# Third norm of a macaron block: two of four tiles scaled by ScalarE, and the next group's additions to x placed ahead of the reciprocals on VectorE

## The chip, the cores and the metric

The kernel runs on one core of one Trainium2 chip. Time is device microseconds of one execution, and the figure of a kernel is the median of its runs. The engines are named as the profile names them: PE is TensorE's matmul stream and PEld its weight loads, DVE is VectorE, ACT is ScalarE, POOL is GpSimd, SP is SyncE. Each engine takes its own instructions strictly in the order in which they were written and waits on semaphores of the others.

## The reference

The input x has 4096 tokens of 256 numbers. Three residual stages follow each other:

```
x = x + 0.5 * moe_ffn(layernorm(x))      # gate, top 2 of 8 experts
x = x + attention(layernorm(x))          # 16 heads, causal
x = x + 0.5 * moe_ffn(layernorm(x))      # the same weights again

layernorm(x) = (x - mean(x)) / sqrt(var(x) + 1e-5)
```

The change is in the third layernorm, the one between the attention and the second pass through the experts. What it computes stays as it is.

## The kernel before

The tokens stand in 32 tiles of 128 (one token per partition), and x stays in SBUF as `x_res`. A norm goes through the tiles in 8 groups of four. In the third norm each group g goes through these steps:

- TensorE projects the heads' output, `attended(g)` on TensorE (line 1484): 16 matmuls of a group, 8 for each of its two pairs of tiles, into banks 4 and 5.
- VectorE adds each pair to x (`attended(g)` on VectorE, which calls `add_pair`, line 1846): two instructions of 128x512. A pair's addition waits for that pair's last matmul.
- VectorE's `statistics` (lines 1514, 1517, 1519): bn_stats and bn_aggr for each of four tiles, then variance plus epsilon for the group.
- ScalarE takes the square root (`sqrt_of`, line 879).
- VectorE's `normalise` takes the reciprocal (line 1524) and scales the four tiles into `rows_of(1)` (line 1536).
- TensorE transposes the four tiles (`transpose_rows`, line 1144): eight transposes, the first feature half of the four tiles and then the second half. ScalarE copies both halves to `feat` (`copy_feat`, line 896).
- TensorE computes the gate logits from `feat` (`gate`, line 1157, 16 matmuls), ScalarE adds the bias (`copy_gate`, line 904), and TensorE turns the logits back (`gate_rows`, line 1166).

The order on TensorE is written out in its `layer_norm`: attended(0), and then for each g attended(g + 1), gate(g - 1), the transposes of g, gate_rows(g - 1). At the end gate(7) and gate_rows(7). On VectorE it is, for each group in turn, additions, statistics, normalise, so that normalise(g) stands ahead of the additions of g + 1. Inside VectorE's `attended` two instructions of the last head's division are written as well: a reciprocal (line 1865) behind the additions of group 1 and a multiplication (line 1869) behind those of group 3. On ScalarE, for each g: copy_gate(g - 1), copy_feat(g), sqrt_of(g + 1).

The first norm has the form that the change brings to the third. There VectorE computes -mean * rstd (line 1527, semaphore `shift`), scales the first two tiles of a group itself, and ScalarE scales the last two (line 922, semaphore `normed_s`) with that value as bias. Behind the third norm `route(1)` chooses the experts, and it needs the gate logits of all groups. SP meanwhile loads the experts' weights, which waits for the last division.

Of the kernel before, what the change touches and what calls it, by code (L numbers as in the profile page):

```python
# [10 lines left out]
ACT = mybir.ActivationFunctionType  # L11
# [5 lines left out]
D = 256  # L17
# [34 lines left out]
LN_GRP = (4, 4, 4)  # L52

BY_SCALAR = 2
# [8 lines left out]
GATES = NT // GATE_TILES  # L63
# [295 lines left out]
def macaron_block(nc, x_in, w_qkv_t, w_out_t, gate_w, gate_b, w1, w2, w3, bias_cols, out):  # L359
    with ExitStack() as ctx:  # L360
        sig = Signals(nc, ctx)

        def sb(name, shape, dt=F32):
            return ctx.enter_context(nc.sbuf_tensor(name, shape, dt))


        x_res = sb("x_res", [P, NT, D])
        rows = sb("rows", [P, NT, ROW])
# [7 lines left out]
        rstd = sb("rstd", [P, 3, NT])  # L376
# [129 lines left out]
        def rows_of(f):  # L506
            return late_rows if f else rows
# [21 lines left out]
        def bc(ap, axis, shape):  # L529
            return ap.unsqueeze(axis).to_broadcast(shape)  # L530
# [4 lines left out]
        s_places, s_steps, S_ALL = bank_places()  # L535
# [326 lines left out]
        def _(eng):  # L862
            need = Waits(eng)
# [12 lines left out]
            def sqrt_of(n, g):  # L876
                a, b = g * LN_GRP[n], (g + 1) * LN_GRP[n]
                need.wait_ge(sig.eps[n], g + 1)
                eng.activation(rstd[:, 1, a:b], rstd[:, 0, a:b], ACT.Sqrt).then_inc(sig.sqrt[n], 1)

            def copy_feat(n, g):

                a, b = g * LN_GRP[n], (g + 1) * LN_GRP[n]
                if n == 1:
                    need.wait_ge(sig.combined[0], 2 * b - NT)
                if n == 2:
                    need.wait_ge(sig.out_mm, b * KD)
                for i0 in range(a, b, 4):
                    for k in range(KD):
                        m = i0 // 4 * KD + k  # L890
                        need.wait_ge(sig.tr[n], 4 * (m + 1))
                        to, of = feat[:, k, i0 * P:(i0 + 4) * P], bank[k][:, :]
                        if n == 1:
                            to = to.rearrange("p (i g b) -> p g i b", i=TPJ, g=TPJ)
                            of = of.rearrange("p (g i b) -> p g i b", i=TPJ, g=TPJ)
                        eng.activation(to, of, ACT.Copy).then_inc(sig.feat[n], 1)
# [10 lines left out]
            def widen_ids(f):  # L907
# [4 lines left out]
                eng.activation(lo_wide[f], bc(lo_ids[:, :], 2, [P, P, HOTS]), ACT.Copy).then_inc(sig.widened[f], 1)  # L912
                eng.activation(hi_wide[f], bc(hi_ids[:, :], 2, [P, N_SUB, HOTS]), ACT.Copy).then_inc(sig.widened[f], 1)

            def first_norm():
                sqrt_of(0, 0)
                for m in range(GATES):
                    if m + 1 < GATES:
                        sqrt_of(0, m + 1)
                    need.wait_ge(sig.shift, m + 1)  # L920
                    for i in range((m + 1) * LN_GRP[0] - BY_SCALAR, (m + 1) * LN_GRP[0]):
                        eng.activation(rows[:, i, 0:D], x_res[:, i, :], ACT.Identity, scale=rstd[:, 0, i:i + 1],
                                       bias=rstd[:, 2, i:i + 1]).then_inc(sig.normed_s, 1)
                    if m:
                        copy_feat(0, m - 1)
                    if m > 1:
                        copy_gate(0, m - 2)
                copy_feat(0, GATES - 1)
                copy_gate(0, GATES - 2)
                copy_gate(0, GATES - 1)  # L930

            def layer_norm(n, add, consume):
                add(0)
                sqrt_of(n, 0)
                groups = NT // LN_GRP[n]
                for g in range(groups):
                    if g + 1 < groups:
                        add(g + 1)
                    if n == 2 and g:
                        copy_gate(1, g - 1)  # L940
                    copy_feat(n, g)
                    if g + 1 < groups:
                        sqrt_of(n, g + 1)
                    consume(g)
                if n == 2:
                    copy_gate(1, GATES - 1)
# [175 lines left out]
        def _(eng):  # L1122
            need = Waits(eng)

            def transpose_rows(n, g):
                need.wait_ge(sig.const, ident_at[0])
                for i0 in range(g * LN_GRP[n], (g + 1) * LN_GRP[n], 4):
                    for k in range(KD):
                        m = i0 // 4 * KD + k
                        need.wait_ge(sig.feat[n], m - 1)  # L1130
                        if n == 1:
                            need.wait_ge(sig.xt_copy[0], DIRECT)
                            need.wait_ge(sig.w_copy, PAIRS)
                        if n == 2:
                            need.wait_ge(sig.s_done, S_ALL)
                        for i in range(i0, i0 + 4):
                            by_vector = LN_GRP[0] - BY_SCALAR
                            if n:
                                need.wait_ge(sig.normed[n], i + 1)
                            elif i - i0 < by_vector:  # L1140
                                need.wait_ge(sig.normed[0], g * by_vector + i - i0 + 1)
                            else:
                                need.wait_ge(sig.normed_s, g * BY_SCALAR + i - i0 - by_vector + 1)
                            eng.transpose(bank[k][:, (i - i0) * P:(i - i0 + 1) * P], rows_of(n // 2)[:, i, k * P:(k + 1) * P],
                                          ident[:, :]).then_inc(sig.tr[n], 1)

# [354 lines left out]
        def _(eng):  # L1501
            need = Waits(eng)

            def statistics(n, g):
                a, b = g * LN_GRP[n], (g + 1) * LN_GRP[n]
                tiles = range(a, b)
                for i in tiles:
                    if n == 0:
                        need.wait_ge(sig.block_loaded[g], 16)
                    elif n == 1:  # L1510
                        need.wait_ge(sig.x_added[0], i // 2 + 1)
                    else:
                        need.wait_ge(sig.attended, i // 2 + 1)
                    eng.bn_stats(stats[:, i, :], x_res[:, i, :]).then_inc(sig.stat[n], 1)  # L1514
                need.wait_ge(sig.stat[n], b)
                for i in tiles:
                    eng.bn_aggr(mean_var[:, i, :], stats[:, i, :]).then_inc(sig.mv[n], 1)
                need.wait_ge(sig.mv[n], b)
                eng.tensor_scalar(rstd[:, 0, a:b], mean_var[:, a:b, 1], EPS, None, ALU.add).then_inc(sig.eps[n], 1)

            def normalise(n, g):
                a, b = g * LN_GRP[n], (g + 1) * LN_GRP[n]
                need.wait_ge(sig.sqrt[n], g + 1)
                eng.reciprocal(rstd[:, 0, a:b], rstd[:, 1, a:b]).then_inc(sig.rstd[n], 1)
                need.wait_ge(sig.rstd[n], g + 1)
                if n == 0:
                    eng.scalar_tensor_tensor(rstd[:, 2, a:b], mean_var[:, a:b, 0], -1.0, rstd[:, 0, a:b], ALU.mult,
                                             ALU.mult).then_inc(sig.shift, 1)
                    b -= BY_SCALAR

                if n == 1:
                    need.wait_ge(sig.table[0], 16 * GROUPS)
                if n == 2:
                    need.wait_ge(sig.s_full, S_ALL)
                for i in range(a, b):
                    eng.tensor_scalar(rows_of(n // 2)[:, i, 0:D], x_res[:, i, :], mean_var[:, i, 0:1], rstd[:, 0, i:i + 1],  # L1536
                                      ALU.subtract, ALU.mult).then_inc(sig.normed[n], 1)
# [8 lines left out]
            def layer_norm(n, add, consume):  # L1546
                add(0)
                statistics(n, 0)
                normalise(n, 0)
                groups = NT // LN_GRP[n]  # L1550
                for g in range(groups):
                    if g + 1 < groups:
                        add(g + 1)
                        statistics(n, g + 1)
                        normalise(n, g + 1)
                    consume(g)

# [379 lines left out]
def bank_places():  # L1937


    places, value, by_place = {}, 0, []  # L1940
    for what, n in attention_steps():
        if what in ("begin_chunk", "probs"):
            value += what != "begin_chunk"
            places[what, n] = len(by_place), value
            by_place.append((what, n))
    return places, by_place, value
# [52 lines left out]
```

## Time and profile before

| | us |
|---|---|
| median of 3 runs | 2087.17 (2084.46 to 2088.4) |
| profiled execution, device time | 2089.44 |
| its span | 2087.7 |
| third norm and its gate, in the span | from 1786 to 1834 |

In the span PE was busy 96% of the time, DVE 88% and ACT 74%. The clock granted to TensorE was 0.975 of full speed in the mean. Instructions are placed in time from the start of the span. A PE instruction's end is modelled and its start is recorded, so the distances between starts are the surer reading. Where a row merges several instructions of one line ("x4"), its duration goes from the first start to the last end, and consecutive instructions overlap slightly.

### The profile page before, as it was taken

Reading aid. Unit: us, or ns where it says so; the run is one execution under the profiler, and the core shown is the slowest. Engines: PE = TensorE matmul, PEld = TensorE weight load, DVE = VectorE, ACT = ScalarE, POOL = GpSimd, SP = SyncE. Lnnn points to the kernel's source line nnn. Section 1 sums busy time; section 2 is a strip of 40 time slices with the busy share of each in tenths; the row PEclk is TensorE's granted clock in tenths of the full one; section 3 lists DMA queues with packets and bytes.
Section 4 is the critical chain, followed back from the end, with each engine's and each line's share of the span. In section 5 each row is a group of like instructions: output and inputs, shape, how many; then the busy total and the mean of one; then the engine's idle time right before and its main releaser. Section 6 shows DMA issues by size and latency. Waiting matters only on the chain.

```text
span 2087.7 us, 99148 instructions
## 1 busy us (share of the span) xinstructions
PE 2005.4 (96%) x43237; PEld 1552.1 (74%) x43237; DVE 1836.2 (88%) x3799; ACT 1545.8 (74%) x3191; POOL 394.2 (19%) x990
## 2 busy tenths in 40 slices
PE   5899989999999999999999999999999999969998
PEld 3788865477777777777777777777877886748885
DVE  6677766899999999999999999999999997667776
ACT  6233346699999999999999999999999998433332
POOL 1343213311111111111111111111111111024330
PEclk8799989999999999999999999999999999969998
DMA  8577603401010010100122001010010102437774
GB/s 273 137 171 172 151 32 122 135 30 37 13 43 21 30 36 12 43 22 29 38 67 72 21 29 37 12 43 22 28 37 12 43 17 67 145 112 176 170 175 131
DMA packets 272403, 154.57 MB, mean 74 GB/s; under 512 B 160142, under 2 KB 253984, under 8 KB 271968
## 3 DMA queue, kind: packets, MB, share of 16 engines
q1 hardware_dynamic: 258764, 119.63, 21.1%
q0 software_dynamic: 6816, 19.20, 3.5%
q10 hardware_dynamic: 6388, 9.39, 1.7%
q8 instruction: 339, 5.55, 1.1%
q14 instruction: 96, 0.79, 0.1%
HBM read 96.98 MB, written 50.93 MB: 71 GB/s over the span
## 4 chain that ended last, share of the span: by engine, by line
PE 82%; DVE 9%; issue 3%; DMA 2%; ACT 1%; POOL 1%; SPq 1%; another core or an unknown queue 0%; DVEq 0%; ACTq 0%; POOLq 0%
PE bank L1387 38%; PE bank L1380 21%; PE bank L1259 16%; PE bank L1469 3%; DVE work L1905 2%; DVE stats L1514 1%; PE bank L1430 1%; DVE x_res L1846 1%; DMA phase<-head_reciprocals 1%; DVE work L1536 0%; POOL phase L660 0%; DVE work L1806 0%; PE bank L1340 0%; POOL work L660 0%
## 5 line engine op out<-in xcount | busy, mean ns | idle before, releaser
L1102 ACT ACTIVATE feat<-bank 128x512 f32<-128x512 f32 (+3 forms) x2304 | 1263.8, 565 | 117.5 <-PE bank L1387 18.1
L1387 PE MATMUL bank<-work 96*32 96x512 bf16 (+2 forms) x15872 | 1211.5, 370 | 7.1 <-DVE work L1905 6.0
L1905 DVE TENSOR_REDUCE work<-bank 128x1 f32<-128x512 f32 (+1 forms) x1920 | 1185.7, 664 | 33.1 <-PE bank L1387 29.4
L1380 PE MATMUL bank<-feat,phase 128*17 128x128 f32 (+3 forms) x18432 | 888.1, 263 | 1.4 <-issue 1.2
L1380 PEld LDWEIGHTS bank<-feat,phase 128*17 128x17 f32 x18432 | 603.0, 98 | 258.8 <-ACT feat L1108 15.7
L1387 PEld LDWEIGHTS bank<-work 96*32 96x32 bf16 (+1 forms) x15872 | 482.3, 96 | 60.0 <-DVE work L1905 26.4
L1259 PE MATMUL bank<-work 128*128 128x256 f32 (+1 forms) x1872 | 384.1, 364 | 11.2 <-ACT work L1008 6.1
L1259 PEld LDWEIGHTS bank<-work 128*128 128x128 f32 x1872 | 329.8, 191 | 60.4 <-issue 15.3
L694 POOL TENSOR_SCALAR_AFFINE_SELECT feat<-feat 128x128 f32<-128x128 f32 x512 | 147.3, 296 | 660.0 <-ACT feat L1102 640.8
L647 POOL DMA_INDIRECT work<-token_table,row_no x142 | 149.9, 1056 | 258.2 <-DVE work L1783 163.1
L1767 DVE COPY work<-phase 128x514 f32 x234 | 101.1, 434 | 82.0 <-ACT work L1008 41.7
L1469 PE MATMUL bank<-work 98*32 98x256 bf16 (+11 forms) x2560 | 171.3, 258 | 0.2 <-ACT feat L1102 0.2
L1008 ACT ACTIVATE work<-bank,work 128x256 f32<-128x256 f32 (+1 forms) x156 | 62.5, 451 | 137.3 <-PE bank L1259 116.9
L685 POOL CAST work<-work 128x4 bf16<-128x4 f32 x128 | 24.0, 188 | 524.5 <-DVE work L1911 522.4
L975 ACT ACTIVATE work<-work 128x256 f32<-128x256 f32 (+1 forms) x156 | 60.6, 389 | 82.3 <-DVE work L1797 70.7
L1469 PEld LDWEIGHTS bank<-work 98*32 98x32 bf16 x2560 | 88.8, 95 | 4.8 <-ACT feat L1102 2.1
L1896 DVE TENSOR_REDUCE work<-bank 128x4 f32<-128x512 f32 x128 | 88.1, 688 | 0.0
L1901 DVE TENSOR_REDUCE work<-bank 128x4 f32<-128x512 f32 x128 | 87.5, 684 | 0.0
L1806 DVE TENSOR_SCALAR work<-bank,work 128x256 f32<-128x256 f32 (+1 forms) x156 | 64.5, 454 | 22.1 <-PE bank L1259 12.6
L1797 DVE SCALAR_TENSOR_TENSOR work<-bank,work 128x256 f32<-128x256 f32 (+1 forms) x156 | 64.3, 453 | 13.3 <-PE bank L1259 10.5
L1430 PEld LDWEIGHTS bank<-work 96*32 96x32 bf16 x2048 | 43.3, 96 | 12.3 <-issue 2.6
L1788 DVE STREAM_TRANSPOSE work<-rows 128x512 f32<-128x512 f32 (+1 forms) x70 | 46.1, 659 | 0.4 <-DMA rows<-tile_rows 0.4
(210 smaller groups left out, 1119.1 us busy)
## 6 DMA issues: line engine op xcount, KB each, us to landing
tile_rows<-work SPq DMA_DIRECT2D x128, 128.0 KB
rows<-tile_rows SPq DMA_DIRECT2D x232, 64.0 KB
phase<-in_w SPq DMA_DIRECT2D x12, 1024.0 KB, 11.9
work<-qk_parts SPq DMA_DIRECT2D x60, 192.0 KB
work<-work SPq DMA_DIRECT2D x512, 0.5 KB
head_sums<-feat SPq DMA_DIRECT2D x128, 64.0 KB
qk_parts<-phase SPq DMA_DIRECT2D x20, 384.0 KB, 2.7
work<-qk_parts SPq DMA_DIRECT2D x60, 128.0 KB
```

The source lines that it names most:

```text
L647: eng.indirect_dma_start(out=x_slot[:, j % NXG, u, :], out_offset=None, in_=table[f], in_offset=bass.IndirectOffsetOnAxis(ap=row_no[:, n:n ...
L694: eng.affine_select(out=tile, in_=tile, compare_op=ALU.is_ge, fill=0.0, base=0, pattern=[[way, P]], channel_multiplier=-way).then_inc(sig. ...
L1102: eng.activation(p_ring[:, n % P_RING, lo:QB], s_bank("probs", n)[:, lo:QB], ACT.Exp, scale=HD ** -0.5).then_inc(sig.s_done, 1)
L1259: mm = eng.matmul(bank[bk][:, m * TILE:m * TILE + WIDTH[j]], staged[:, b, l, k * D + m * P:k * D + (m + 1) * P], act, start=(k == 0), stop ...
L1380: mm = eng.matmul(bank[ACC_BANK][GRID * g:GRID * g + VW, GRID * i0:P], v_aug[:, t, h, :], weights[:, i0:TPJ, g, :], start=(t == 0), stop=( ...
L1387: mm = eng.matmul(out[GRID * g:GRID * (g + 1), width], left[:, GRID * g:GRID * (g + 1)], right, start=start, stop=stop)
L1469: mm = eng.matmul(s_bank("probs", n)[own, part], keys[:, own], queries[:, part], start=True, stop=True)
L1767: eng.tensor_copy(staged[:, j % 2, l, :], experts[:, bass.ds(expert_of[j], 1), l, :].rearrange("p a w -> p (a w)"),).then_inc(sig.staged[f ...
L1806: eng.tensor_scalar(acts[:, 2, j % 2, m, 0:WIDTH[j]], bank[BANKS_OF[j][1]][:, m * TILE:m * TILE + WIDTH[j]], staged[:, j % 2, 1, KD * D + ...
L1896: eng.tensor_reduce(maxima[:, h % 2, j, :, DIAGONAL_AT], scores[:, 0:QB].rearrange("p (i s) -> p i s", i=TPJ), AX_X, ALU.max).then_inc(sig ...
L1901: eng.tensor_reduce(short[:, at - 1:at + 3], scores[:, 0:QB].rearrange("p (i s) -> p i s", i=TPJ), AX_X, ALU.max).then_inc(sig.a_done, 1)
L1905: eng.tensor_reduce(maxima[:, h % 2, j, PLACE[i], at:at + 1], scores[:, 0:hi - lo], AX_X, ALU.max).then_inc(sig.a_done, 1)
```

## The change

In the third norm VectorE now computes -mean * rstd too and scales two tiles of each group, and ScalarE scales the other two in `scale_rows`, behind sqrt_of of the same group. VectorE's order becomes: additions(0), statistics(0), and then for each g additions(g + 1), normalise(g), statistics(g + 1). TensorE's order is unchanged; only the semaphores that its transposes wait for are changed to match. The first and the second norm execute the same instructions in the same order as before.

```
             def layer_norm(n, add, consume):        # ScalarE
                 add(0)
                 sqrt_of(n, 0)
+                if n == 2:
+                    scale_rows(n, 0)
...
                     if g + 1 < groups:
                         sqrt_of(n, g + 1)
+                        if n == 2:
+                            scale_rows(n, g + 1)

+            def scale_rows(n, g):                   # ScalarE
+                need.wait_ge(sig.shift, n // 2 * GATES + g + 1)
+                if n == 2:
+                    need.wait_ge(sig.s_full, S_ALL)
+                for i in range((g + 1) * LN_GRP[n] - BY_SCALAR, (g + 1) * LN_GRP[n]):
+                    eng.activation(rows_of(n // 2)[:, i, 0:D], x_res[:, i, :], ACT.Identity, scale=rstd[:, 0, i:i + 1],
+                                   bias=rstd[:, 2, i:i + 1]).then_inc(sig.normed_s, 1)

                 need.wait_ge(sig.rstd[n], g + 1)    # VectorE, normalise
-                if n == 0:
+                if n != 1:
                     eng.scalar_tensor_tensor(rstd[:, 2, a:b], mean_var[:, a:b, 0], -1.0, rstd[:, 0, a:b], ALU.mult,
                                              ALU.mult).then_inc(sig.shift, 1)
                     b -= BY_SCALAR

             def layer_norm(n, add, consume):        # VectorE
                 add(0)
                 statistics(n, 0)
-                normalise(n, 0)
                 groups = NT // LN_GRP[n]
+                if n == 1:
+                    normalise(n, 0)
                 for g in range(groups):
                     if g + 1 < groups:
                         add(g + 1)
+                    if n == 2:
+                        normalise(n, g)
+                    if g + 1 < groups:
                         statistics(n, g + 1)
+                    if n == 1 and g + 1 < groups:
                         normalise(n, g + 1)
                     consume(g)
```

## Rows read from the trace of the kernel before

**Rows 1.** The chain of waits in one period: start us, us, what.
```profile
1815.18 1.19 DVE x_res L1846 x2
1816.37 1.32 DVE stats L1514 x4
...
1818.13 0.18 DVE rstd L1519
...
1818.58 0.19 DVE rstd L1524
1818.79 1.38 DVE work L1536 x4
```

**Rows 2.** Busy time by stretch: PE, PEld, DVE, ACT, POOL, clock, DMA.
```profile
1815.00:1820.00 5.00, 5.00 (x42) 4.12 (x34) 4.62 (x17) 1.66 (x4) 0.00 (x0) 1.00 1.09 357
...
1830.00:1831.00 1.00, 1.00 (x5) 0.86 (x6) 0.15 (x1) 0.22 (x1) 0.00 (x0) 0.50 0.00 0
```

**Rows 3.** Timeline of PE: start, us, instructions, idle before.
```profile
1786.19 7.14 PE L1484 MATMUL bank<-w_out_sb,rows 128*128 128x256 f32 x32 [0.49 <-DVE rows L1869]
1793.58 1.64 PE L1144 MATMUL bank<-ident,work 128*128 128x128 f32 x8 [0.25 <-DVE work L1536]
1795.14 3.69 PE L1484 MATMUL bank<-w_out_sb,rows 128*128 128x256 f32 x16
...
1805.69 3.70 PE L1484 MATMUL bank<-w_out_sb,rows 128*128 128x256 f32 x16
1809.32 0.64 PE L1157 MATMUL bank<-feat,gate_w_sb 128*32 128x128 f32 x16
1809.89 1.11 PE L1144 MATMUL bank<-ident,work 128*128 128x128 f32 x8
1810.84 0.31 PE L1166 MATMUL bank<-ident,v_rest 128*128 128x32 f32 x2
1810.98 3.70 PE L1484 MATMUL bank<-w_out_sb,rows 128*128 128x256 f32 x16
...
1821.54 3.70 PE L1484 MATMUL bank<-w_out_sb,rows 128*128 128x256 f32 x16
...
1829.24 2.29 PE L1144 MATMUL bank<-ident,work 128*128 128x128 f32 x8 [0.97 <-DVE work L1536]
```

**Rows 4.** Timeline of DVE in the third norm, with the same columns.
```profile
1789.91 0.69 DVE L1846 TENSOR_TENSOR x_res<-x_res,bank 128x512 f32<-128x512 f32 x1 [1.04 <-PE bank L1484]
1790.52 1.40 DVE L1514 BATCH_NORM_STATS2 stats<-x_res 128x6 f32<-128x256 f32 x4
1795.52 0.34 DVE L1865 RECIPROCAL work<-work 128x32 f32<-128x32 f32 x1
1805.70 0.68 DVE L1869 TENSOR_TENSOR rows<-rows,feat 128x512 f32<-128x512 f32 x1
1808.80 1.38 DVE L1536 TENSOR_SCALAR work<-x_res,mean_var,rstd 128x256 f32<-128x256 f32 x4
1828.78 1.38 DVE L1536 TENSOR_SCALAR work<-x_res,mean_var,rstd 128x256 f32<-128x256 f32 x4
```

**Rows 5.** Timeline of DVE, ACT and PE in the first norm.
```profile
18.02 0.17 DVE L1524 RECIPROCAL rstd<-rstd 128x4 f32<-128x4 f32 x1
18.22 0.16 DVE L1527 SCALAR_TENSOR_TENSOR rstd<-mean_var,rstd 128x4 f32<-128x4 f32 x1
18.30 0.73 DVE L1536 TENSOR_SCALAR rows<-x_res,mean_var,rstd 128x256 f32<-128x256 f32 x2
18.42 1.09 ACT L922 ACTIVATE rows<-x_res,rstd 128x256 f32<-128x256 f32 x2
18.95 1.40 DVE L1514 BATCH_NORM_STATS2 stats<-x_res 128x6 f32<-128x256 f32 x4
...
22.90 1.14 PE L1144 MATMUL bank<-ident,rows 128*128 128x128 f32 x8 [0.80 <-ACT feat L896]
```

**Rows 6.** Groups by line and form over the span, one of ACT.
```profile
L975 ACT ACTIVATE work<-work 128x256 f32<-128x256 f32 x128 | 52.2, 408 | 68.5 <-DVE work L1797 57.0 <-issue 10.9 <-ACT work L989 0.7
```

More of the change, by code:

```diff
@@ L919, in first_norm @@
                         sqrt_of(0, m + 1)
[L920 to L923, printed above, removed]
+                    scale_rows(0, m)
                     if m:
@@ L1137, in transpose_rows @@
                             by_vector = LN_GRP[0] - BY_SCALAR
-                            if n:
-                                need.wait_ge(sig.normed[n], i + 1)
+                            if n == 1:
+                                need.wait_ge(sig.normed[1], i + 1)
                             elif i - i0 < by_vector:
-                                need.wait_ge(sig.normed[0], g * by_vector + i - i0 + 1)
+                                need.wait_ge(sig.normed[n], g * by_vector + i - i0 + 1)
                             else:
-                                need.wait_ge(sig.normed_s, g * BY_SCALAR + i - i0 - by_vector + 1)
+                                need.wait_ge(sig.normed_s, (n // 2 * GATES + g) * BY_SCALAR + i - i0 - by_vector + 1)
                             eng.transpose(bank[k][:, (i - i0) * P:(i - i0 + 1) * P], rows_of(n // 2)[:, i, k * P:(k + 1) * P],
@@ L1548, in layer_norm @@
                 statistics(n, 0)
-                normalise(n, 0)
                 groups = NT // LN_GRP[n]
+                if n == 1:
+                    normalise(n, 0)
                 for g in range(groups):
```

## The prediction

> **What bounds the kernel now.** I began with the chain of waits, cut down to the third norm. It runs almost wholly through VectorE: additions, statistics, a short trip to ScalarE for the root, reciprocal, scaling, then the next additions [rows 1]. Read alone, it says that VectorE sets the pace and that work taken off it is time won. So I looked at TensorE next. In the 5 us from 1815 it was busy for all 5.00, at the full granted clock (1.00), and VectorE for 4.62 [rows 2]. Busy time on PE is modelled, so the starts have to decide. Call S the start of a group's output projection. S goes from 1805.69 to 1810.98 (5.29), and from 1795.14 to 1821.54 in five periods, 5.28 each [rows 3]. VectorE's scalings start at 1808.80 and 1818.79, 5.00 a period [rows 1, 4]; in the one period with the last division it had 0.60 more. PE's pitch showed none of that 0.60. Its pitch is the sum of its own work: projection 3.63, gate 0.57, eight transposes 0.95, gate_rows 0.14, together 5.29, each read from one start to the next [rows 3]. Both engines are nearly full, and PE, which never waits, is the one that sets the pitch. VectorE is just ahead: it starts scaling group g at S + 3.11 [rows 3, 4] (S of group g + 1's projection) while PE is still in that projection, and PE wants the first scaled tile at S + 4.20. With 0.46 from the start of a scaling to the transpose that it releases (1828.78 to 1829.24 [rows 3, 4]), the slack is 0.63 us.
>
> **The order of the additions.** This is the decisive part. The additions of g + 1 now stand ahead of the reciprocal of g. The second of them waits for the last of the 16 projection matmuls, so normalise(g) can't start before PE has finished the projection, and directly behind the projection PE wants normalise(g)'s result (only gate(g - 1), 0.57, lies between). A pair of operations that ran beside PE becomes a loop through PE. From S:
>
> - last matmul of the projection ends and the second addition starts: + 3.70 [rows 3] (the 1789.91 addition begins as its 16 matmuls end)
> - addition to next instruction: 0.60, as the row from 1789.91 to 1790.52 has it (0.61) [rows 4]; reciprocal at 4.30
> - reciprocal to the -mean * rstd instruction 0.20, that to the first scaling 0.08 [rows 5]: 4.50 and 4.58
> - first transpose 0.46 later, at 5.04, where PE was ready at 4.20
> - ScalarE's pair starts 0.20 after the -mean * rstd instruction and takes 1.09 for both [rows 5]; with 0.05 for the semaphore, PE can begin the fourth tile's first transpose at 5.84
> - five transposes are left from there: 5 x 0.119 = 0.59; gate_rows 0.14 (its bias copy on ScalarE, queued behind the two scalings, takes 0.37 and ends near 6.2, ahead of it). The next projection starts at 6.57.
>
> The pitch goes from 5.28 to 6.57, so each regular period loses 1.29. ScalarE's last tile sets it, not VectorE's second. Nothing else on VectorE is late: statistics(g) now start at 5.23 and end about 2 us later, some 0.8 us into the next projection, whose first pair is ready only at 1.9. The root and its wait are hidden there too. That is the gain of the change, and it buys idle time on VectorE.
>
> **Head.** Group 0's normalise started at once behind its statistics; now it waits for both projections, which end at 1786.19 + 7.14 = 1793.33 [rows 3]. Then addition 0.60, the last head's reciprocal (0.34 long, some 0.26 to the next [rows 4]), reciprocal, 0.28 to the scaling: ScalarE's tiles are ready at 1794.39 + 0.20 + 1.09 + 0.05 = 1795.73, and group 2's projection starts 0.59 later at 1796.32, against 1795.14 [rows 3]: + 1.2.
>
> **The division.** Line 1869 (0.60 to the next instruction) stands behind the additions of group 3, now also between projection and normalise(2), so that it goes onto the loop once: + 0.60. Its data was there without a wait at 1805.70; the reciprocal that starts the transfers comes 1.6 us earlier now and the multiplication about 1 us later. SP's load of the experts' weights waits for this multiplication and slips by the same 1 us; it has finished around 1827, and the first expert tile is some 40 us later. I cost that at nothing; without this cover it would be that 1 us.
>
> **Tail.** From S of the last projection, normalise(6) goes as above, and the last statistics start at 4.58 + 0.65 = 5.23 [rows 5]. Start of statistics to reciprocal is 1818.58 - 1816.37 = 2.21 [rows 1], then 0.20: -mean * rstd at 7.64, and ScalarE's second tile is usable at 7.64 + 0.20 + 1.09 + 0.05 = 8.98. Before, VectorE's four scalings began at 1828.78 = S + 7.24 and the last was usable at 7.24 + 1.38 + 0.05 = 8.67 [rows 3, 4]. That is + 0.3. ScalarE's root of group 7 stands behind its two copies of group 6, which by my count now end about when the root is due; for that I add 0.1. Tail: + 0.4. The granted clock was 0.50 from 1830 [rows 2], after PE had waited; I leave it there.
>
> **Sum.** 1.2 + 5 x 1.29 + 0.60 + 0.4 = 8.6 us. The profiled execution took 2089.44 with a span of 2087.70, 2.27 above the median of the runs; it would become 2098.1, and against the median 2087.17 the forecast is 2095.8. Everything behind the norm depends on its last gate logits and moves as a whole.
>
> **Bounds.** The ScalarE instruction is priced from the first norm, where transfers into SBUF were busy. The nearest other row is a 128x256 activation of 408 ns [rows 6] against the 1.09 for two (0.59 one, 0.50 apart). At 0.33 apart and 0.41 long, the pair takes 0.74, VectorE's own tiles then set nearly the same point, and a period loses 0.95: in all 1.7 us less, with the same effect on head and tail another 0.7 less. Above: an addition of its whole 0.69 before the next instruction, and a release 0.1 slower than the 0.46 that I read once, give 0.19 more a period, 1.3 in all. The tail at full clock would give back about 1.2 (the transposes took 2.29 there and 1.11 at 1809.89 [rows 3]), or cost 1 if it fell earlier. So + 5.0 to + 11, and runs of the kernel before spread by 2 us around their median.
>
> **Rivals.**
>
> *VectorE sets the pace, faster.* By the chain's reading a period of VectorE loses two scalings (1.38 - 0.65 = 0.73) and the wait for the root (about 0.25), and gains 0.07: 0.91 less in seven periods, 6.4 us, 2080.8. It holds if PE's 5.28 is stretched by VectorE, and decides where PE's true work per group is under 4.4. The chain [rows 1] speaks for it; that PE kept 5.28 when VectorE took 0.60 more speaks against. Chance 0.04. The Trainium skill, in Perfetto Trace Analysis, Identifying the Most-Contended Engine, speaks for this rival: matmul busy time is no good measure, one should look at weight-load busy time and the matmul rate, and occupancy is right for the other engines. By it PE stands at 4.12 of 5 here and VectorE at 4.62, and VectorE is the engine to relieve. Distances of starts don't have the fault that it warns of, and they say PE.
>
> *The loop is shorter than I make it, no measurable change.* If the faster ScalarE, a tail at full clock and a favourable clock afterwards come together: 8.6 - 2.4 - 1.2 - 1 = 4.0, 2091.2. For it speaks that the clock changes several times in the routing stage behind the norm. Chance 0.10.
>
> *The clock falls inside the norm.* PE would wait 1.3 us in each 6.6. Once at 0.50, a group's projection goes from 3.43 of matmuls to twice that and the transposes from 1.11 to 2.29 [rows 3]: up to 4 us a period, some 2111 if it lasted, and 2100 for one or two periods. Against it: in the first norm PE waited 0.80 before a group's transposes too, and they took 1.14, the time of full clock [rows 5]. Chance 0.06.
>
> **How the numbers follow.** The forecast has 0.80. About 0.2% (4.2 us) is what a measurement of this kernel can tell from no change. The forecast's own range, 2092 to 2099, lies almost wholly beyond + 4.2; slower gets 0.86 (forecast and the clock), same 0.10, faster 0.04. The range goes down to 2090, into the second rival and the spread of medians, and up to 2100.
>
> **What would show it.** In the profile after, output projections should start 6.4 to 6.7 us apart, with transposes held for about 0.85 us by VectorE's or ScalarE's scaling and PE idle there. VectorE should wait for line 1484 at its additions, which it did not do in the middle of the norm. The last projection should start near 1829.8. If PE's pitch is below 5.5, the loop isn't there and I am wrong; if it is 6.2, ScalarE's price was; if it is over 7, the clock.

## The result: slower by 9.3 us, and the profile after

The changed kernel took 2096.5 us in the median of five runs (2092.66 to 2097.36), against 2087.17 for the kernel before in the same comparison. The ratio is 1.0043, with a 95% interval from 1.0028 to 1.0059. The forecast was 2095.8. Run once more later on another chip, it took 2100.23 against 2092.17 for the kernel before there, a ratio of 1.0034 (1.0020 to 1.0047).

The profiled execution has a span of 2095.2 us, 7.5 longer. In it the third norm starts 1.11 us earlier than before. The change touches no work ahead of it, and between two profiles of the changed kernel this start differs by 3.06 us (1785.08 here, 1788.14 in the later one). From the first output projection to the first reduction of the routing it takes 56.11 us, against 48.28: + 7.83. What lies behind takes 254.01 against 253.23: + 0.78. These three make up the 7.5.

The timeline of PE in the changed kernel, beside [rows 3]. The projection has line 1493 now, the gate 1166, the transposes 1153, gate_rows 1175.

```profile
1785.08 7.14 PE L1493 MATMUL bank<-w_out_sb,rows 128*128 128x256 f32 x32 [0.49 <-ACT feat L1117]
1793.92 1.48 PE L1153 MATMUL bank<-ident,work 128*128 128x128 f32 x8 [1.69 <-DVE work L1545]
1795.23 3.62 PE L1493 MATMUL bank<-w_out_sb,rows 128*128 128x256 f32 x16
...
1801.79 3.70 PE L1493 MATMUL bank<-w_out_sb,rows 128*128 128x256 f32 x16
...
1807.48 1.57 PE L1153 MATMUL bank<-ident,work 128*128 128x128 f32 x8 [1.42 <-DVE work L1545]
...
1809.02 3.70 PE L1493 MATMUL bank<-w_out_sb,rows 128*128 128x256 f32 x16
...
1815.66 3.70 PE L1493 MATMUL bank<-w_out_sb,rows 128*128 128x256 f32 x16
1819.29 0.64 PE L1166 MATMUL bank<-feat,gate_w_sb 128*32 128x128 f32 x16
1820.75 1.57 PE L1153 MATMUL bank<-ident,work 128*128 128x128 f32 x8 [0.82 <-DVE work L1545]
1822.15 0.31 PE L1175 MATMUL bank<-ident,v_rest 128*128 128x32 f32 x2
1822.30 3.70 PE L1493 MATMUL bank<-w_out_sb,rows 128*128 128x256 f32 x16
...
1828.93 3.70 PE L1493 MATMUL bank<-w_out_sb,rows 128*128 128x256 f32 x16
...
1837.25 1.57 PE L1153 MATMUL bank<-ident,work 128*128 128x128 f32 x8 [0.22 <-DVE work L1545]
```

Read the starts first. From 1815.66 to 1822.30 a period is 6.64 us; it was 5.28. Then read the brackets. The work itself is unchanged (3.70, 0.64), but ahead of the transposes PE sits idle for 0.82 us until a scaling of VectorE releases it, and they then take 1.57 where [rows 3] has 1.11. They are fed tile by tile, as the weight loads of the same transposes show:

```profile
1821.07 0.20 PEld L1153 LDWEIGHTS bank<-ident,work 128*128 128x128 f32 x2 [0.18 <-DVE work L1545]
...
1821.55 0.53 PEld L1153 LDWEIGHTS bank<-ident,work 128*128 128x128 f32 x5 [0.28 <-ACT work L920]
```

ScalarE's second tile releases the last five. In the period with the last division (1801.79 to 1809.02, 7.23) the idle time is 1.42.

The timeline of DVE and ACT in the same period. Before, VectorE had no idle time at its additions in the middle of the norm; the first line is from that kernel.

```profile
1815.09 1.28 DVE L1846 TENSOR_TENSOR x_res<-x_res,bank 128x512 f32<-128x512 f32 x2
```

```profile
1817.67 0.69 DVE L1860 TENSOR_TENSOR x_res<-x_res,bank 128x512 f32<-128x512 f32 x1 [1.36 <-PE bank L1493]
1819.40 0.69 DVE L1860 TENSOR_TENSOR x_res<-x_res,bank 128x512 f32<-128x512 f32 x1 [1.04 <-PE bank L1493]
1820.00 0.17 DVE L1533 RECIPROCAL rstd<-rstd 128x4 f32<-128x4 f32 x1
1820.21 0.16 DVE L1536 SCALAR_TENSOR_TENSOR rstd<-mean_var,rstd 128x4 f32<-128x4 f32 x1
1820.29 0.73 DVE L1545 TENSOR_SCALAR work<-x_res,mean_var,rstd 128x256 f32<-128x256 f32 x2
...
1820.40 1.09 ACT L920 ACTIVATE work<-x_res,rstd 128x256 f32<-128x256 f32 x2 [3.85 <-DVE rstd L1536]
```

The second addition starts at 1819.40, 0.11 us after PE has gone on to the gate, and the scaling that PE's next transposes need is queued behind it. VectorE is idle for 2.40 us of each period. It was relieved, and the relief became waiting.

The chain of waits, which ran through VectorE alone in [rows 1], now alternates:

```profile
1819.40 0.69 DVE x_res L1860
...
1820.21 0.16 DVE rstd L1536
1820.37 0.34 DVE work L1545
...
1820.75 0.76 PE bank L1153 x3
...
1821.55 0.77 PE bank L1153 x5
...
1822.46 3.55 PE bank L1493 x16
```

### The profile page after: what moved, and what is told of

Its sections match the earlier page's. It is cut to its first block, busy times and chain, and to the rows that moved or that the text cites. A ratio compares the mean times of both kernels' runs of the same rounds, so it can differ in the third digit from the quotient of the medians.

```text
span 2095.2 us, 99155 instructions
## 1 busy us (share of the span) xinstructions
PE 2008.9 (96%) x43237; PEld 1540.6 (74%) x43237; DVE 1831.9 (87%) x3791; ACT 1552.0 (74%) x3207; POOL 394.7 (19%) x990
## 4 chain that ended last, share of the span: by engine, by line
PE 83%; DVE 8%; issue 3%; DMA 2%; POOL 1%; ACT 1%; SPq 1%; DVEq 0%; ACTq 0%; POOLq 0%
PE bank L1396 38%; PE bank L1389 21%; PE bank L1268 15%; PE bank L1478 3%; DVE work L1919 2%; PE bank L1493 1%; PE bank L1439 1%; PE bank L1153 1%; DVE x_res L1860 1%; DVE stats L1523 1%; DMA rows<-tile_rows 0%; DVE work L1820 0%; POOL phase L660 0%; POOL work L660 0%; PE bank L1349 0%
## 5 line engine op out<-in xcount | busy, mean ns | idle before, releaser
L1389 PEld LDWEIGHTS bank<-feat,phase 128*17 128x17 f32 x18432 | 591.7, 98 | 267.3 <-ACT feat L1117 15.6
L1396 PEld LDWEIGHTS bank<-work 96*32 96x32 bf16 (+1 forms) x15872 | 475.5, 96 | 62.3 <-DVE work L1919 27.5
L1811 DVE SCALAR_TENSOR_TENSOR work<-bank,work 128x256 f32<-128x256 f32 (+1 forms) x156 | 64.4, 454 | 14.4 <-PE bank L1268 11.4
```

Source lines behind the costliest of these rows:

```text
L1389: mm = eng.matmul(bank[ACC_BANK][GRID * g:GRID * g + VW, GRID * i0:P], v_aug[:, t, h, :], weights[:, i0:TPJ, g, :], start=(t == 0), stop=( ...
L1396: mm = eng.matmul(out[GRID * g:GRID * (g + 1), width], left[:, GRID * g:GRID * (g + 1)], right, start=start, stop=stop)
```

## Experiments

All times in this table come from the profiled execution of each kernel, in us from the start of its first output projection. "Tail" is from the start of the last projection to the routing's first reduction, and "stage" is the sum. The medians of e1 to e4 stand beside 2086.17 for the kernel before, those of e6 to e8 beside 2092.17 on another chip.

| kernel | last projection starts | tail | stage | regular pitch |
|---|---|---|---|---|
| before | 35.35 | 12.93 | 48.28 | 5.28 |
| changed | 43.85 | 12.26 | 56.11 | 6.64 |
| e1_split_only | 35.09 | 11.33 | 46.42 | 5.28 |
| e2_order_only | 44.42 | 12.93 | 57.35 | 6.73 |
| e3_between | 35.30 | 11.34 | 46.64 | 5.27 |
| e4_ahead | 32.78 | 14.13 | 46.91 | 5.27 |
| e7_e3_ahead | 32.52 | 13.83 | 46.35 | 5.28 |
| e6_tail | 32.47 | 12.16 | 44.63 | 5.32 |
| e8_changed_again | 45.53 | 12.26 | 57.79 | 6.64 |

The theory was that the order of the additions makes a loop through TensorE. The rivals were ScalarE's share in the scaling, and VectorE as the engine that had set the pace.

### The two halves of the change, each alone

e1_split_only is the changed kernel with VectorE's old order:

```
...
                 for g in range(groups):
                     if g + 1 < groups:
                         add(g + 1)
-                    if n == 2:
-                        normalise(n, g)
-                    if g + 1 < groups:
                         statistics(n, g + 1)
-                    if n == 1 and g + 1 < groups:
                         normalise(n, g + 1)
```

> ScalarE scales two of four tiles as in the changed kernel, but VectorE keeps the order of the kernel before (additions, statistics, normalise of one group). Theory (the additions ahead of the reciprocals make a loop through TensorE; the split itself is harmless): output projections start 5.28 us apart as before, TensorE never waits in the middle, the norm with its gate (first projection to the first reduction of the routing) takes 46.5 to 47.7 us against 48.3 before and 56.1 changed, because only the tail gets shorter by the two scalings; time 2085 to 2087. Rival A (ScalarE's scaling is what is late, since its queue holds copies too): pitch above 6 us, time near 2095. Rival B (VectorE sets the pace of the kernel before): VectorE has about 0.7 us a group less, so the pitch falls to about 4.4 us and the time to about 2081.

e2_order_only is the kernel before with VectorE's new order and nothing else:

```
                 add(0)
                 statistics(n, 0)
-                normalise(n, 0)
...
                     if g + 1 < groups:
                         add(g + 1)
+                    if n == 2:
+                        normalise(n, g)
+                    if g + 1 < groups:
                         statistics(n, g + 1)
...
```

> The additions of the next group stand ahead of the reciprocals as in the changed kernel, but VectorE scales all four tiles. Theory: the loop is there in full; fourth tile usable at 4.51 + 1.38 + 0.05 = 5.94 us behind the start of the projection (5.84 with the split), pitch 6.7 us, tail 0.7 us longer, the stage about 57 us, time 2096 to 2098. Rival A (ScalarE's scaling is the cost): without it the time returns to within 2 us of before, pitch 5.3 to 5.6.

Measured: e1_split_only 2082.47 us, ratio to before 0.9988 (0.9976 to 0.9999). e2_order_only 2097.19 us, ratio 1.0054 (1.0037 to 1.0071). The first lies 2.5 us below the range that was expected, its stage (46.42) just below; the second is in its range. The timeline of e1_split_only, PE and DVE:

```profile
1811.31 3.70 PE L1493 MATMUL bank<-w_out_sb,rows 128*128 128x256 f32 x16
...
1813.60 0.68 DVE L1855 TENSOR_TENSOR x_res<-x_res,bank 128x512 f32<-128x512 f32 x1
...
1815.05 0.69 DVE L1855 TENSOR_TENSOR x_res<-x_res,bank 128x512 f32<-128x512 f32 x1 [0.77 <-PE bank L1493]
1815.52 1.09 PE L1153 MATMUL bank<-ident,work 128*128 128x128 f32 x8
...
1816.59 3.70 PE L1493 MATMUL bank<-w_out_sb,rows 128*128 128x256 f32 x16
```

VectorE now waits 0.77 us for PE in each regular period and 0.17 in the one with the division, and the pitch still is 5.28 in all of them, with no idle bracket at PE's transposes. So VectorE did not set the pace of the periods before, and that rival falls. It did bound the end: ahead of the last transposes PE waited 0.97 us for VectorE's scaling before [rows 3], and waits 0.64 here. ScalarE's share isn't late either. And the timeline of e2_order_only, where ScalarE scales nothing:

```profile
1815.89 3.70 PE L1484 MATMUL bank<-w_out_sb,rows 128*128 128x256 f32 x16
...
1822.62 3.70 PE L1484 MATMUL bank<-w_out_sb,rows 128*128 128x256 f32 x16
```

Pitch 6.73: the whole loss is there without the split. The order costs 9.1 us of the stage by itself (57.35 - 48.28). The split is worth 1.2 us with the new order (57.35 - 56.11) and 1.9 with the old one (48.28 - 46.42). Both differences to the kernel before hold a difference of the clock in the tail, which by the estimate below is 1.1 us: at the same clock the order would cost about 10.2 and the split save about 0.7.

### Is it the order, or the wait of one instruction?

e3_between is the changed kernel with normalise(g) between the two additions of group g + 1 (normalise(7) stays behind the last statistics):

```
             def attended(g):
                 for i2 in range(g * LN_GRP[2], (g + 1) * LN_GRP[2], 2):
                     need.wait_ge(sig.out_mm, KD * (i2 + 2))
                     add_pair(i2, 4 + i2 // 2 % 2, sig.attended)
+                    if g and i2 == g * LN_GRP[2]:
+                        normalise(2, g - 1)
...
-                    if n == 2:
+                    if n == 2 and g + 1 == groups:
                         normalise(n, g)
```

> Changed kernel, with normalise(g) written between the two additions of group g + 1 instead of behind both. Only the second addition waits for the projection's last matmul. Theory (it is the wait of the second addition that puts the scaling onto the loop, not the order as such): scaling starts about 2.9 us behind the start of the projection, TensorE wants it at 4.20, so the pitch is 5.28 us again, the division no longer shows, stage 46.5 to 47.7 us, time 2085 to 2087. Rival (any addition ahead of the reciprocal costs, or two engines sharing the scaling do): pitch above 6.

Measured: 2083.41 us (expected 2085 to 2087), ratio 0.9986 (0.9971 to 1.0000). The timeline of DVE and PE in the group after the first:

```profile
1792.33 0.69 DVE L1860 TENSOR_TENSOR x_res<-x_res,bank 128x512 f32<-128x512 f32 x1 [0.33 <-PE bank L1493]
1792.94 0.17 DVE L1533 RECIPROCAL rstd<-rstd 128x4 f32<-128x4 f32 x1
...
1793.22 0.73 DVE L1545 TENSOR_SCALAR work<-x_res,mean_var,rstd 128x256 f32<-128x256 f32 x2
...
1794.06 0.69 DVE L1860 TENSOR_TENSOR x_res<-x_res,bank 128x512 f32<-128x512 f32 x1
1794.53 1.09 PE L1153 MATMUL bank<-ident,work 128*128 128x128 f32 x8
```

The place of one addition, behind normalise instead of ahead of it, brings the stage from 56.11 back to 46.64. An addition ahead of the reciprocal is harmless; the one that waits for the projection's last matmul is not. The division's 0.60 no longer shows in PE's pitch either; it stands behind the second addition and so behind the scaling.

### A group of slack on TensorE

e4_ahead keeps VectorE's order of the change and lets TensorE project one group further ahead of its transposes:

```
             def layer_norm(n, add, consume):        # TensorE
                 add(0)
+                add(1)
                 groups = NT // LN_GRP[n]
                 for g in range(groups):
-                    if g + 1 < groups:
-                        add(g + 1)
+                    if g + 2 < groups:
+                        add(g + 2)
...
                     if g + 1 < groups:              # ScalarE
                         add(g + 1)
+                        sqrt_of(n, g + 1)
                     if n == 2 and g:
                         copy_gate(1, g - 1)
+                    if g + 1 < groups:
+                        scale_rows(n, g + 1)
                     copy_feat(n, g)
-                    if g + 1 < groups:
-                        sqrt_of(n, g + 1)
-                        if n == 2:
-                            scale_rows(n, g + 1)
```

> Changed kernel, with TensorE's output projections one group further ahead of its transposes (and ScalarE's root and scaling ahead of the copies to match). The loop gets a whole group of slack. Theory (TensorE's own work of 5.28 us a group is the floor of the stage, and the loop is the only loss): no wait of TensorE in the middle, last projection starts about 32.7 us behind the first (35.4 before, 43.8 changed), tail 12.3 as in the changed kernel, stage about 45 us, 3 us less than before: 2083 to 2085. Rival B (VectorE sets the pace): the pitch stays above 5.3 with VectorE never idle. Rival C (the loop only moves, into the wait of a projection for its bank): projections wait for additions, stage above 48.

Measured: 2084.4 us, ratio 0.9996 (0.9984 to 1.0009). The pitch and the last projection (32.78) came as expected, the stage didn't (46.91 against 45). The tail grew to 14.13, and I had left out two things. One is plain work: with the last projection a group earlier, one group more of gate, transposes and gate_rows comes behind it, 1.64 us by the starts (1813.22 to 1814.86). So tails with and without this edit can't be compared, and the stage decides. The other is in the timeline of ACT and PE:

```profile
1819.61 1.09 ACT L920 ACTIVATE work<-x_res,rstd 128x256 f32<-128x256 f32 x2
...
1820.61 1.06 ACT L896 ACTIVATE feat<-bank 128x512 f32<-128x512 f32 x2
...
1821.72 0.64 PE L1165 MATMUL bank<-feat,gate_w_sb 128*32 128x128 f32 x16 [1.41 <-ACT feat L896]
```

PE's gate waits 1.41 us, twice, for copies that stand behind ScalarE's scaling. In the middle of the norm no gate waits, since a projection stands between the copies and the gate; once the projections are over nothing does. In the changed kernel the two waits of this kind in the tail were 0.66 and 0.65.

e7_e3_ahead puts the same two edits on e3_between, to see whether VectorE's scaling of group 6 ahead of the last statistics made the tail.

> e3_between with only the projections one group further ahead and ScalarE's order of e4_ahead. The gates of the last groups still wait for copies behind ScalarE's scaling: last projection at 32.7, tail 12.8 to 14 us, stage 46 to 47 us. If the tail is near 11.5 instead, e4_ahead's long tail came from VectorE's scaling of group 6 between the last addition and the last statistics.

Its tail is 13.83 and its stage 46.35 (one run, 2093.91 us). So VectorE's scaling did not make the long tail. Of the 2.5 us more than e3_between's 11.34, 1.64 are the group of TensorE's work, and two gates wait 1.27 us each for copies (1830.26 and 1833.34), where e3_between's wait 0.66 and 0.65. That ScalarE's order makes these waits is read from the trace, where the copies start as the scaling ends; e6_tail changes that order, but TensorE's with it, so it wasn't tried alone.

e6_tail has e3_between's VectorE, the projections a group ahead, transposes ahead of the gates, and the last groups in another order on two engines (the calls, in sequence):

```
# TensorE, g from 0 to 5, then the rest
    add(g + 2); transpose_rows(n, g); [g = 5: transpose_rows(n, 6)]; gate(1, g - 1); gate_rows(1, g - 2)
    gate(1, 5); gate_rows(1, 4); transpose_rows(n, 7); gate(1, 6); gate_rows(1, 5); gate_rows(1, 6)
    gate(1, 7); gate_rows(1, 7)
# ScalarE, g from 0 to 5, then the rest
    sqrt_of(n, g + 1); scale_rows(n, g + 1); copy_feat(n, g); [g < 5: copy_gate(1, g - 1)]
    copy_feat(n, 6); sqrt_of(n, 7); copy_gate(1, 4); scale_rows(n, 7); copy_gate(1, 5)
    copy_feat(n, 7); copy_gate(1, 6); copy_gate(1, 7)
```

> normalise(g) between the two additions of g + 1 and the split over two engines as in e3_between, output projections one group further ahead on TensorE as in e4_ahead, and the last groups reordered: transposes of group 6 directly behind those of 5, the gates of 4 and 5 behind them, ScalarE's copies of a group ahead of the root and scaling that would hold them up. Theory (e4_ahead had its last projection early, 32.8 us behind the first, and lost it in a tail of 14.1 us, because the gates waited for copies that stood behind ScalarE's scaling): no such wait is left, last projection at 32.7, tail about 11.4, stage 44.2 us, about 2 us less than e1_split_only's 46.4 and 4 less than before: 2082 to 2083. Rival (the tail is bound by TensorE's own work of the last two groups): tail 12.5 or more, stage above 45.2.

Measured: 2088.36 us beside 2092.17 for the kernel before on that chip, ratio 0.9979 (0.9967 to 0.9990). Its stage is the shortest of the series; its time is not clear of e1_split_only's and e3_between's, whose intervals overlap with this one. The timeline of PE and DVE:

```profile
1787.89 10.78 PE L1497 MATMUL bank<-w_out_sb,rows 128*128 128x256 f32 x48 [0.49 <-ACT feat L1116]
...
1820.36 3.70 PE L1497 MATMUL bank<-w_out_sb,rows 128*128 128x256 f32 x16
...
1832.52 0.42 DVE L1602 TENSOR_REDUCE per_expert<-bank 128x8 f32<-128x256 f32 x1 [4.28 <-PE bank L1174]
```

The stage is 44.63, 3.65 less than before, with a tail of 12.16 where I expected 11.4. Of the 0.8 between them about 0.6 is at gate(7): its last copy ended at 1830.28 and it started at 1830.94, where gate(7) of the changed kernel started 0.05 after its copy. I had put it behind gate_rows(6), which waits for a bias copy of ScalarE (1830.18 to 1830.55); another order wasn't tried.

### The changed kernel again

> The changed kernel once more beside the others: pitch 6.6 us, stage 56.1 us. With the clock full in the tail as in its first profile (12.3 us behind the start of the last projection); a tail at 0.50 would add about 1.5 us. Time 8 to 10 us above the kernel before.

Measured: 2100.23 us, 8.1 above the kernel before, ratio 1.0034 (1.0020 to 1.0047). The pitch is 6.64 again, but the stage was 57.79, not 56.1. One projection took 5.39 us. The timeline of PE, and then the busy time by stretch (PE, PEld, DVE, ACT, POOL, granted clock, DMA):

```profile
1804.85 3.70 PE L1493 MATMUL bank<-w_out_sb,rows 128*128 128x256 f32 x16
...
1812.08 5.39 PE L1493 MATMUL bank<-w_out_sb,rows 128*128 128x256 f32 x16
```

```profile
1810.00:1812.00 2.00, 1.42 (x10) 1.00 (x10) 2.00 (x7) 1.58 (x4) 0.00 (x0) 1.00 0.33 62
...
1813.00:1814.00 1.00, 1.00 (x4) 0.76 (x3) 0.00 (x0) 0.00 (x0) 0.00 (x0) 0.50 1.09 387
...
1816.00:1817.00 1.00, 1.00 (x6) 0.88 (x5) 0.12 (x1) 0.00 (x0) 0.00 (x0) 1.00 1.05 347
```

The granted clock went to 0.50 (1.2 GHz) behind the period with the longest idle time, PE's 1.42 us around the division, and was back at 1.00 in 1816. It cost 1.7 us (8.32 us for the period, against 6.64), which is the whole difference of the two stages. That is my third rival, in one period of one execution. In the first profile of the same kernel the clock stayed at 1.00 behind the same 1.42 us.

## Why the prediction was right, step by step

- **What bounds the kernel.** TensorE at 5.28 us a group: shown by e1_split_only, in which VectorE got slack and the pitch stayed. The slack of 0.63 us in the prediction is that of one period, just behind the last division; two periods on it is 1.21 (scaling at 1818.79, projection at 1816.26), as VectorE's 5.00 against 5.28 implies.
- **The loop.** Pitch forecast 6.57, measured 6.64, and 6.73 without ScalarE, where the new order alone is on trial. Its joints: second addition at 3.74 behind the start of the projection (3.70), scaling at 4.63 (4.58), first transpose at 5.09 (5.04), and 1.40 from there to gate_rows (1.39). ScalarE's pair takes the 1.09 that it was priced at, and its second tile releases the transposes at 5.89 (5.84), so the smaller loss by a faster ScalarE didn't come. e3_between shows that it is the second addition's wait.
- **Head.** + 1.2 forecast, and measured: the third projection starts 10.15 us behind the first, 8.95 before.
- **Division.** + 0.60 forecast; its period is 7.23 against 6.64, + 0.59.
- **Tail.** This term was mis-sized: + 0.4 forecast, - 0.67 measured. The order of events was right (first transpose of group 7 at 8.32 behind the last projection's start, 7.64 + 0.08 + 0.46 = 8.18 by my numbers). Half of that small difference is a misreading: I took 2.21 us from statistics to reciprocal out of the chain, and by the starts in the timeline it is 2.28. But I had left the clock at 0.50. It stayed at full speed, as this stretch of the changed kernel shows:

```profile
1838.00:1840.00 2.00, 1.31 (x24) 1.17 (x23) 0.00 (x0) 1.33 (x3) 0.00 (x0) 1.00 0.00 0
```

  In [rows 2] it was 0.50 from 1830, before the last transposes had ended. What that cost can be estimated with e2_order_only, which executes the same instructions from there on as the kernel before, at 1.00: from the start of the last transposes to the routing's first reduction it takes 4.11 us (1838.17 to 1842.28), the kernel before 5.23 (1829.24 to 1834.47). With these 1.12 taken off, the tail before is 11.81 and the change adds 0.45, the 0.4 of the forecast. The work was sized right and the clock was not; I had this gain of 1.2 us in the bounds, not in the sum. Why the clock fell before and not after wasn't tried and stays open. The length of the waits doesn't sort the cases: it fell behind 0.65 and 0.97 us in the kernel before, and stayed at 1.00 behind 1.27 twice in e7_e3_ahead. No single profile settles such a term.
- **Sum.** 8.6 forecast; in the traces 1.20 + 7.30 - 0.67 = 7.83 (7.30 for the five periods, 7.05 forecast). The medians gave 9.3 in the first comparison and 8.1 in the later one (about 7 by its ratio of 1.0034). That the median came within 0.7 us of the forecast is in part luck: the periods lost 0.25 more than forecast, the tail 1.07 less, and 0.78 came in behind the norm, where I had nothing.

By its busy time VectorE had the higher share (4.62 in 5 us, against 4.12 of PE's weight loads), and giving it 0.77 us of slack a period left PE's pitch at 5.28. The rule of the Trainium skill that I had weighed (Perfetto Trace Analysis, Identifying the Most-Contended Engine), by which VectorE was the engine to relieve, and this measurement differ, and the measurement decides.

## What to carry to other kernels

When an instruction is moved up in an in-order queue, look at what it waits for: ahead of the reciprocal, an addition that waits for the last matmul of a block turns work that ran beside the block into work behind it. Take the pace of a pair of nearly full engines from the distances between the starts of one engine's recurring instruction, and check them in a period in which the other had more to do. Put the instruction with the late wait last, and look at the tail apart: an order that a long operation covers in the middle has no cover there.

## What the runs showed of the hardware

TensorE's granted clock fell to half in the middle of the norm in one of two profiles of the same kernel, behind 1.42 us of idle time. It cost 1.7 us there; in the other profile the clock stayed at 1.00 behind the same idle time. ScalarE's scaling with a per-partition scale and bias took 1.09 us for two tiles in every period, with the transfers of the expert weights running (355 GB/s from 1816 to 1822.5 in the changed kernel) or not yet begun (0 GB/s from 1800 to 1804), and the same in the first norm; so transfers don't set its price here.
